# A curvature-flow stage on one core: another split of its small steps between the engines

## The chip, the cores and the metric

The kernel runs on 1 core of a Trainium2 chip. The metric is the device time in microseconds (us), the median of the runs. TensorE (PE) multiplies 32-row blocks held in SBUF and adds into PSUM (`bank`, 8 banks), VectorE (DVE) and ScalarE (ACT) do elementwise work on both memories, GpSimd (POOL) does elementwise work on SBUF, and SyncE (SP) issues the DMAs.

## The reference

Four layers follow one another on a batch of 16 images with 16 channels of 32 x 32: an attention layer, two residual convolution layers, and the curvature flow that the change is about. Its part of the reference, cut:

```python
def step(u, _):                                  # 10 steps; c() clips to +-10
    ux, uy, uxx, uxy, uyy = _derivs(u)           # Sobel stencils, each through c()
    g2 = ux * ux + uy * uy
    denK = jnp.maximum(1.0 + g2, EPS)
    K = jnp.clip((uxx * uyy - uxy * uxy) / (denK * denK + EPS), -5.0, 5.0)
    denH = jnp.sqrt(1.0 + g2 + EPS)
    H = ((1.0 + uy * uy) * uxx - 2.0 * ux * uy * uxy + (1.0 + ux * ux) * uyy) / (2.0 * denH ** 3 + EPS)
    H = jnp.clip(H, -5.0, 5.0)
    u = u + DT * jnp.clip(alpha * K + beta * H, -1.0, 1.0)      # DT = 0.01
    return jnp.pad(u[:, :, 1:-1, 1:-1], ((0, 0), (0, 0), (1, 1), (1, 1)), mode='edge'), None
u, _ = jax.lax.scan(step, x, None, length=10)
return 0.7 * u + 0.3 * x
```

## The kernel before

Until about 412 us the kernel streams weights and does the attention and the convolutions; the change leaves that alone but for a few two-element constants. Then the flow runs. The images are cut by channels into 4 chunks (`NCH`), each a tile `u[c]` of 128 partitions (4 channels of 32 image rows) by 34 x 16 columns (image column, batch). 10 steps of 4 chunks make 40 **slots**. A slot's inner part has 30 x 16 = 480 columns (`NF`); where two fields are handled at once, an instruction has 960.

**TensorE.** A derivative is a sum of terms, each a 32 x 32 matrix (the vertical part) times a shifted view of `u` (the horizontal part). `stencil` (line 585) does one term as 4 matmuls on 4 of the array's 32 x 32 tiles; `add` (line 596) does the same for a pointwise sum. This text calls such a group of 4 a **round**. Round t reads partitions shifted by 32 t: t = 0 is `u` itself, t = 1 to 3 are copies `turned`, which SyncE makes by six DMAs per slot (`turn`, line 357) after the border columns of `u` are written. Rounds of one t use the same four tiles and follow one another; rounds of different t use different tiles. A slot has 22 rounds: UX 2 (t = 0), UY 3 and UXX 3 (t = 1), UXY 4 (t = 2), UYY 5 (t = 3), and 5 adds (t = 0): ONE, ONE, MINUS_TWO sum the numerator of H in the second bank of the slot's bank pair, where UX stood before; ALPHA and BETA sum the step in bank 7.

**Per slot on the other engines**, by the line numbers of the profile:
- DVE: clip of ux, uy (L930, 960 columns), clip of the step in two instructions, L934 in PSUM and L939 with the addition to `u`, K's product `khk` (L944), clip of uxy (L947), H's product `khh` (L952), clip of uxx, uyy (L957, 960), `slope` = 1 + ux^2 + uy^2 (L961), `outer` (L963, 960).
- ACT: three squares (L1074 `p2`, L1075 `sqr` of 960, L1077 `sqxy`), the clip of H as two ramps (L1080, L1082), then the powers of the slope: Ln, Square, Exp (L1085, L1086, L1088), two Ln (L1090, L1092), two Exp (L1095 `invk`, L1097 `invh`).
- POOL: the products `cxy` (L1144), `m` (L1155), `cross` (L1158), `num` (L1161), the clip of K (L1147), and the copy of the two border columns of `u` (L1151), which SP waits for.

Every engine works its list in the order written; a slot's work is spread over iterations k, k+1 and k+2 of `slot_step` (new, old, older). After the loop, `edge` matmuls (L683) and `finish` (L981, L985) form 0.7 u + 0.3 x.

## Time and profile before

| | |
|---|---|
| median of 3 runs | 716.74 us (716.69 to 717.53) |
| the profiled execution, its own time | 716.67 us |
| span of its trace | 714.9 us |
| busy: PE, DVE, ACT, POOL | 643.1, 408.9, 328.2, 237.3 us |
| the flow, first stencil matmul to the end | 415.7 to 714.9 us |

In a timeline row stand the start and the duration in us, the engine, the line, the operation, the tiles written and read and their shape, and in brackets the idle time before it with the instruction that ended it. The start of one instruction to the start of the next on its engine is often shorter than the duration, as instructions overlap at their ends.

### The profile page before, as it was taken

How to read it: one execution, taken by the hardware profiler on the slowest of the kernel's cores; microseconds unless marked ns; L12 is line 12 of the kernel's file. 1: busy time of each engine (PE TensorE's matmuls, PEld its weight loads, DVE VectorE, ACT ScalarE, POOL GpSimd, SP SyncE). 2: the span in 40 equal slices, each digit the busy share in tenths (PEclk: the TensorE clock that was granted, in tenths of full speed). 3: DMA queues.
4: the chain of work that ended last, by engine and by line, in shares of the span. 5: the costliest groups of instructions: out<-in, count | busy, mean ns of one | idle time of the engine just before them, and what ended most of it. 6: DMA issues, size and time to landing. Idle time of an engine off the chain costs nothing.

```text
span 714.9 us, 22856 instructions
## 1 busy us (share of the span) xinstructions
PE 643.1 (90%) x10128; PEld 402.9 (56%) x10128; DVE 408.9 (57%) x635; ACT 328.2 (46%) x622; POOL 237.3 (33%) x250
## 2 busy tenths in 40 slices
...
GB/s 372 424 402 407 429 426 426 425 428 426 427 427 422 427 428 427 425 428 425 427 427 297 143 165 97 122 120 121 120 120 126 115 121 120 128 113 128 113 98 61
...
## 3 DMA queue, kind: packets, MB, share of 16 engines
...
q14 instruction: 11, 0.09, 0.0%
...
## 4 chain that ended last, share of the span: by engine, by line
PE 69%; DMA 25%; DVE 4%; issue 1%; ACT 1%; SPq 0%; DVEq 0%; ACTq 0%
PE bank L592 29%; DMA ring<-wout_w 15%; PE bank L600 11%; PE bank L402 8%; PE bank L418 7%; PE bank L526 4%; PE bank L471 4%; DMA ring<-wqk_p 3%; DMA ring<-wout_p 3%; DMA ring<-wv_w 3%; PE bank L552 3%; DMA xw<-x_window 1%; PE bank L557 1%; DVE reg_g L709 1%; PE bank L445 1%
## 5 line engine op out<-in xcount | busy, mean ns | idle before, releaser
L592 PE MATMUL bank<-ring 32*32 32x480 f32 x4800 | 283.5, 568 | 1.3 <-DMA ring<-reg_a 1.3
L600 PE MATMUL bank<-ring 32*32 32x480 f32 x1600 | 186.2, 564 | 1.2 <-ACT ring L1082 0.8
L592 PEld LDWEIGHTS bank<-ring 32*32 32x32 f32 x4800 | 125.3, 103 | 39.4 <-issue 25.7
L1144 POOL TENSOR_TENSOR ring<-ring 128x480 f32<-128x480 f32 x40 | 48.8, 1221 | 175.1 <-DVE ring L930 175.1
L418 PE MATMUL bank<-ring,small 128*32 128x256 f32 x1152 | 79.5, 424 | 30.3 <-DMA ring<-wout_w 24.6
L600 PEld LDWEIGHTS bank<-ring 32*32 32x32 f32 x1600 | 77.8, 104 | 37.0 <-issue 11.4
L418 PE MATMUL bank<-ring,xw 128*32 128x256 f32 x1024 | 62.8, 405 | 12.9 <-DMA ring<-wv_w 12.9
L418 PEld LDWEIGHTS bank<-ring,small 128*32 128x32 f32 x1152 | 39.6, 119 | 60.9 <-issue 22.3
L1155 POOL TENSOR_TENSOR ring<-ring 128x480 f32<-128x480 f32 x40 | 48.6, 1215 | 56.9 <-DVE ring L957 56.9
L765 DVE SCALAR_TENSOR_TENSOR reg_a<-bank,prm 128x512 f32<-128x512 f32 x4 | 2.8, 691 | 101.4 <-PE bank L478 101.4
L402 PE MATMUL bank<-reg_a,ring 128*128 128x256 f32 x256 | 57.9, 388 | 2.8 <-DMA ring<-wqk_p 2.0
L418 PEld LDWEIGHTS bank<-ring,xw 128*32 128x32 f32 x1024 | 33.8, 116 | 40.2 <-DMA ring<-wv_w 16.2
L402 PEld LDWEIGHTS bank<-reg_a,ring 128*128 128x128 f32 x256 | 49.6, 195 | 11.3 <-DMA ring<-wqk_p 2.9
L592 PE MATMUL bank<-reg_a,ring 32*32 32x480 f32 x480 | 55.3, 566 | 0.0
L1122 POOL MEMSET reg_d<- 128x2176 f32 x1 | 1.9, 1914 | 147.4 <-PE bank L478 147.4
L914 DVE STREAM_TRANSPOSE reg_b<-bank 128x256 f32<-128x256 f32 x16 | 7.2, 450 | 75.8 <-PE bank L418 75.8
L1158 POOL TENSOR_TENSOR ring<-ring 128x480 f32<-128x480 f32 x40 | 48.7, 1218 | 0.0
L1161 POOL TENSOR_TENSOR ring<-ring 128x480 f32<-128x480 f32 x40 | 48.7, 1217 | 0.0
L930 DVE TENSOR_SCALAR ring<-bank 128x960 f32<-128x960 f32 x40 | 45.8, 1146 | 3.7 <-PE bank L592 3.7
L957 DVE TENSOR_SCALAR ring<-bank 128x960 f32<-128x960 f32 x40 | 45.9, 1147 | 1.5 <-PE bank L592 1.5
L963 DVE SCALAR_TENSOR_TENSOR ring<-bank,ring 128x960 f32<-128x960 f32 x40 | 45.9, 1146 | 0.0
...
## 6 DMA issues: line engine op xcount, KB each, us to landing
...
ring<-reg_a SPq DMA_DIRECT2D x60, 136.0 KB, 2.5
...
```

The lines of the kernel that those rows point to most:

```text
L402: ins = te.matmul(bank[:, 4 + n % 2, (h % 2) * TOK:(h % 2 + 1) * TOK], half[2 * (k % NSLOT) + h // 4][:, c, h % 4 * DH:(h % 4 + 1) * DH], ...
L418: ins = te.matmul(bank[32 * j:32 * j + 32, b_, n0:n0 + 256], lhs(c), slot[k % NSLOT][:, c, 256 * j:256 * j + 256], start=start and c == 0, ...
L471: ins = te.matmul(bank[:, 4 + n % 2, :], fl[:, c, t * P:(t + 1) * P], half[2 * (kv % NSLOT) + h][:, c, :], start=(c == 0), stop=(c == KC - 1))
L592: last = te.matmul(bank[QUAD * j:QUAD * (j + 1), field, 0:NF], mat(m, (j + t) % NCH), whole[at_, 2 + off:S + off, :], start=(n == 0), stop ...
L600: last = te.matmul(bank[at_, to, 0:NF], mat(m, j), from_[at_, :], start=start, stop=stop, skip_group_check=True)
L930: v.tensor_scalar(two(f01[q]), pair(q), 10.0, -10.0, ALU.min, ALU.max).then_inc(ve["clip1"], 1)
L957: v.tensor_scalar(two(f34[q]), bank[:, OUTER:OUTER + 2, 0:NF], 10.0, -10.0, ALU.min, ALU.max).then_inc(ve["clip2"], 1)
L963: v.scalar_tensor_tensor(two(ab[q]), pair(q), 1.0, two(f34[q]), ALU.add, ALU.mult).then_inc(ve["outer"], 1)
L1144: p.tensor_tensor(cxy[q], f01[q][:, 0:NF], f01[q][:, NF:2 * NF], ALU.mult).then_inc(po["cxy"], 1)
L1155: p.tensor_tensor(mxy[q], f34[q][:, 0:NF], f34[q][:, NF:2 * NF], ALU.mult).then_inc(po["m"], 1)
L1158: p.tensor_tensor(cross[q], cxy[q], mix[q], ALU.mult).then_inc(po["cross"], 1)
L1161: p.tensor_tensor(num[q], mxy[q], sqm[q], ALU.subtract).then_inc(po["num"], 1)
```

## The change

All of it is in the flow. TensorE takes the x derivative UX from the copy with t = 2 instead of `u` itself; its rounds, and the instructions of all engines, stand in a new order, in which uxx, uxy's second half and uyy of a slot fall in the iteration behind its ux and uy. The clip of the step moves from DVE's L934 to two ScalarE ramps (`low` out of PSUM, `high` back into it), the clip of H from two ScalarE ramps to one GpSimd instruction, ScalarE's two logarithms become one of 960 columns, and the border copy moves from GpSimd to a `tensor_copy` on VectorE. The loops of VectorE and ScalarE are written out. The diff, cut: the old bodies are those printed above, so only new lines stand here, without the renamed semaphores and constants.

```diff
@@ a name for a position in the order
+class Slot:
+    def __init__(self, k):
+        self.k, self.q, self.live = k, k % 2, 1 <= k <= SLOTS
+        self.i, self.c = (k - 1) // NCH, (k - 1) % NCH
+        self.first = self.i == 0
@@ TensorE: slot_step(k), lines 603-665 replaced
+now, old, older = Slot(k), Slot(k - 1), Slot(k - 2)
+if old.live:
+    te.wait_ge(ld_turn[2][old.c], 32 * (old.i + 1))
+    if old.k > 1:
+        te.wait_ge(ve["clip2"], old.k - 1)
+    stencil(OUTER + 1, old, 3, UYY, 0)
+    stencil(MIXED, old, 2, UXY, 2)
+    if old.k > 1:
+        te.wait_ge(ve["clip2"], old.k - 1)
+    stencil(OUTER, old, 1, UXX, 0)
+    stencil(MIXED, old, 2, UXY, 3).then_inc(pe["fldxy"], 1)
+if older.live:
+    te.wait_ge(ve["outer"], older.k)
+    add(bank_set(older.q) + 1, ONE, ab[older.q][:, 0:NF], True, False)
+if old.live:
+    stencil(OUTER + 1, old, 3, UYY, 1)
+if older.live:
+    add(bank_set(older.q) + 1, ONE, ab[older.q][:, NF:2 * NF], False, False)
+if old.live:
+    stencil(OUTER + 1, old, 3, UYY, 2)
+    stencil(OUTER, old, 1, UXX, 1)
+if older.live:
+    te.wait_ge(po["cross"], older.k)
+    add(bank_set(older.q) + 1, MINUS_TWO, cross[older.q], False, True).then_inc(pe["hn"], 1)
+if old.live:
+    stencil(OUTER + 1, old, 3, UYY, 3)
+if now.live:
+    te.wait_ge(ld_turn[1][now.c], 32 * (now.i + 1))
+    if now.k > 1:
+        te.wait_ge(ve["clipxy"], now.k - 1)
+    stencil(MIXED, now, 2, UXY, 0)
+if old.live:
+    stencil(OUTER, old, 1, UXX, 2)
+    stencil(OUTER + 1, old, 3, UYY, 4).then_inc(pe["fld2"], 1)
+if now.live:
+    stencil(MIXED, now, 2, UXY, 1)
+    te.wait_ge(ld_turn[0][now.c], 32 * (now.i + 1))
+    if now.k > 2:
+        te.wait_ge(ve["khk"], now.k - 2)
+    stencil(bank_set(now.q), now, 1, UY, 0)
+if older.live:
+    te.wait_ge(po["clip_k"], older.k)
+    if older.k > 1:
+        te.wait_ge(ve["u"], older.k - 1)
+    add(STEP, ALPHA, clip_k[older.q], True, False)
+if now.live:
+    if now.k > 2:
+        te.wait_ge(ve["khh"], now.k - 2)
+    elif now.k == 2:
+        te.wait_ge(ac["u_in"], 2)
+    stencil(bank_set(now.q) + 1, now, 2, UX, 0)
+    stencil(bank_set(now.q), now, 1, UY, 1)
+if older.live:
+    te.wait_ge(po["clip_h"], older.k)
+    add(STEP, BETA, clip_h[older.q], False, True).then_inc(pe["step"], 1)
+if now.live:
+    stencil(bank_set(now.q) + 1, now, 2, UX, 1)
+    stencil(bank_set(now.q), now, 1, UY, 2).then_inc(pe["fld1"], 1)
@@ VectorE: lines 895-899
-then(v.tensor_scalar(dt_ab, prm[:, COL["alpha"][0]:COL["beta"][1]], DT, None, ALU.mult))
-then(v.tensor_scalar(five_ab, dt_ab, 5.0, None, ALU.mult))
-then(v.tensor_scalar(ten_ab, five_ab, 2.0, None, ALU.mult))
-then(v.tensor_scalar(neg_b, dt_ab[:, 1:2], -1.0, None, ALU.mult))
-v.tensor_tensor(mid, five_ab[:, 0:1], five_ab[:, 1:2], ALU.add).then_inc(ve["scales"], 1)
+v.tensor_scalar(dt_ab, prm[:, COL["alpha"][0]:COL["beta"][1]], DT, None, ALU.mult).then_inc(ve["scales"], 1)
@@ VectorE: slot_step(k), lines 923-963 replaced
+now, old, older = Slot(k), Slot(k - 1), Slot(k - 2)
+if old.live:
+    v.wait_ge(ac["p2"], old.k)
+    v.wait_ge(ac["sqr"], old.k)
+    v.scalar_tensor_tensor(slope[old.q], pair(old.q)[:, 1, :], 1.0, p2[old.q], ALU.add, ALU.add).then_inc(ve["slope"], 1)
+    v.wait_ge(pe["fld2"], old.k)
+    v.tensor_scalar(two(f34[old.q]), bank[:, OUTER:OUTER + 2, 0:NF], 10.0, -10.0, ALU.min, ALU.max).then_inc(ve["clip2"], 1)
+    v.wait_ge(ve["clip2"], old.k)
+    v.scalar_tensor_tensor(two(ab[old.q]), pair(old.q), 1.0, two(f34[old.q]), ALU.add, ALU.mult).then_inc(ve["outer"], 1)
+if now.live:
+    v.wait_ge(pe["fld1"], now.k)
+    v.tensor_scalar(two(f01[now.q]), pair(now.q), 10.0, -10.0, ALU.min, ALU.max).then_inc(ve["clip1"], 1)
+    v.wait_ge(pe["fldxy"], now.k)
+    v.tensor_scalar(mix[now.q], bank[:, MIXED, 0:NF], 10.0, -10.0, ALU.min, ALU.max).then_inc(ve["clipxy"], 1)
+if older.live:
+    v.wait_ge(ac["high"], older.k)
+    if older.first:
+        v.wait_ge(ac["x3"], older.k)
+    inner = u[older.c][:, 2 * B:S * B]
+    v.scalar_tensor_tensor(inner, bank[:, STEP, 0:NF], DT, inner, ALU.subtract, ALU.add).then_inc(ve["u"], 1)
+if old.live:
+    v.wait_ge(po["num"], old.k)
+    v.wait_ge(ac["invk"], old.k)
+    v.tensor_tensor(kh[old.q][:, 0:NF], num[old.q], pair(old.q)[:, 0, :], ALU.mult).then_inc(ve["khk"], 1)
+if older.live:
+    if older.k <= SLOTS - NCH:
+        v.wait_ge(ve["u"], older.k)
+        image_ = u3(older.c)
+        v.tensor_copy(image_[:, 1:S + 1:S - 1, :], image_[:, 2:S:S - 3, :]).then_inc(ve["pad"], 1)
+if old.live:
+    v.wait_ge(pe["hn"], old.k)
+    v.wait_ge(ac["invh"], old.k)
+    v.tensor_tensor(kh[old.q][:, NF:2 * NF], pair(old.q)[:, 1, :], inv_h[old.q], ALU.mult).then_inc(ve["khh"], 1)
@@ VectorE: lines 988-994 replaced (the Fori loop goes)
+for k in range(1, SLOTS + 2):
+    slot_step(k)
+for x in range(NCH - 1):
+    finish(x)
+slot_step(SLOTS + 2)
@@ ScalarE: slot_step(k), lines 1069-1097 replaced
+now, old, older = Slot(k), Slot(k - 1), Slot(k - 2)
+if old.live:
+    a.wait_ge(ve["clip1"], old.k)
+    a.activation(pair(old.q), f01[old.q].rearrange("p (x n) -> p x n", x=2), ACT.Square).then_inc(ac["sqr"], 1)
+    a.wait_ge(ve["clipxy"], old.k)
+    a.activation(sqm[old.q], mix[old.q], ACT.Square).then_inc(ac["sqxy"], 1)
+    a.wait_ge(ve["slope"], old.k)
+    a.activation(lnw[old.q], slope[old.q], ACT.Ln, bias=D_EPS).then_inc(ac["lnw"], 1)
+    a.wait_ge(ve["slope"], old.k)
+    a.activation(den[old.q][:, 0:NF], slope[old.q], ACT.Square).then_inc(ac["psq"], 1)
+    a.wait_ge(ac["lnw"], old.k)
+    a.activation(den[old.q][:, NF:2 * NF], lnw[old.q], ACT.Exp, bias=LN2, scale=1.5).then_inc(ac["w15"], 1)
+if older.live:
+    a.wait_ge(pe["step"], older.k)
+    a.activation(low[older.q], bank[:, STEP, 0:NF], ACT.Relu, bias=DT, scale=-1.0).then_inc(ac["low"], 1)
+if old.live:
+    a.wait_ge(ac["psq"], old.k)
+    a.wait_ge(ac["w15"], old.k)
+    a.activation(den[old.q], den[old.q], ACT.Ln, bias=D_EPS).then_inc(ac["ln"], 1)
+if older.live:
+    a.wait_ge(ac["low"], older.k)
+    a.activation(bank[:, STEP, 0:NF], low[older.q], ACT.Relu, bias=2 * DT, scale=-1.0).then_inc(ac["high"], 1)
+if now.live:
+    a.wait_ge(ve["clip1"], now.k)
+    a.activation(p2[now.q], f01[now.q][:, 0:NF], ACT.Square).then_inc(ac["p2"], 1)
+if old.live:
+    a.wait_ge(ve["outer"], old.k)
+    a.wait_ge(ac["ln"], old.k)
+    a.activation(pair(old.q)[:, 0, :], den[old.q][:, 0:NF], ACT.Exp, scale=-1.0).then_inc(ac["invk"], 1)
+    a.wait_ge(ac["ln"], old.k)
+    a.activation(inv_h[old.q], den[old.q][:, NF:2 * NF], ACT.Exp, scale=-1.0).then_inc(ac["invh"], 1)
@@ ScalarE: lines 1108-1114 replaced (the Fori loop goes)
+for k in range(1, SLOTS + 3):
+    slot_step(k)
@@ GpSimd: lines 1140-1161 replaced
+now, old = Slot(k), Slot(k - 1)
+if old.live:
+    p.wait_ge(ve["clipxy"], old.k)
+    p.wait_ge(po["cxy"], old.k)
+    p.tensor_tensor(cross[old.q], cxy[old.q], mix[old.q], ALU.mult).then_inc(po["cross"], 1)
+    p.wait_ge(ve["clip2"], old.k)
+    p.tensor_tensor(mxy[old.q], f34[old.q][:, 0:NF], f34[old.q][:, NF:2 * NF], ALU.mult).then_inc(po["m"], 1)
+    p.wait_ge(ac["sqxy"], old.k)
+    p.wait_ge(po["m"], old.k)
+    p.tensor_tensor(num[old.q], mxy[old.q], sqm[old.q], ALU.subtract).then_inc(po["num"], 1)
+if now.live:
+    p.wait_ge(ve["clip1"], now.k)
+    p.tensor_tensor(cxy[now.q], f01[now.q][:, 0:NF], f01[now.q][:, NF:2 * NF], ALU.mult).then_inc(po["cxy"], 1)
+if old.live:
+    p.wait_ge(ve["khk"], old.k)
+    p.tensor_scalar(clip_k[old.q], kh[old.q][:, 0:NF], 5.0, -5.0, ALU.min, ALU.max).then_inc(po["clip_k"], 1)
+    p.wait_ge(ve["khh"], old.k)
+    p.tensor_scalar(clip_h[old.q], kh[old.q][:, NF:2 * NF], 5.0, -5.0, ALU.min, ALU.max).then_inc(po["clip_h"], 1)
+for k in range(1, SLOTS + 2):
+    slot_step(k)
@@ SyncE: line 371
-sp.wait_ge(po["pad"], i * NCH + (c + 1 - NCH))
+sp.wait_ge(ve["pad"], i * NCH + (c + 1 - NCH))
```

## Rows read from the trace of the kernel before

**Rows 1.** Busy time by engine, 540 to 580 us: length, PE, PEld, DVE, ACT, POOL, PEclk, DMA.

```profile
540.00:580.00 40.00, 40.00 (x1008) 26.00 (x998) 38.42 (x53) 37.73 (x69) 31.05 (x34) 1.00 0.44 115
```

**Rows 2.** Timeline of PE, one slot: first UX pass, first ALPHA pass, last MINUS_TWO pass.

```profile
543.66 0.60 PE L592 MATMUL bank<-reg_a,ring 32*32 32x480 f32 x4
...
545.27 0.61 PE L600 MATMUL bank<-ring 32*32 32x480 f32 x4
...
549.32 0.59 PE L600 MATMUL bank<-ring 32*32 32x480 f32 x2
```

**Rows 3.** Timeline of DVE, the same slot.

```profile
542.86 0.66 DVE L952 TENSOR_TENSOR ring<-bank,ring 128x480 f32<-128x480 f32 x1 [0.23 <-PE bank L600]
543.43 1.15 DVE L957 TENSOR_SCALAR ring<-bank 128x960 f32<-128x960 f32 x1
544.50 0.65 DVE L961 SCALAR_TENSOR_TENSOR ring<-bank,ring 128x480 f32<-128x480 f32 x1
545.06 1.15 DVE L963 SCALAR_TENSOR_TENSOR ring<-bank,ring 128x960 f32<-128x960 f32 x1
...
547.19 0.72 DVE L934 TENSOR_SCALAR bank<-bank,small 128x480 f32<-128x480 f32 x1
547.94 0.66 DVE L939 SCALAR_TENSOR_TENSOR reg_a<-bank,reg_a 128x480 f32<-128x480 f32 x1
548.52 0.64 DVE L944 TENSOR_TENSOR ring<-ring,bank 128x480 f32<-128x480 f32 x1
```

**Rows 4.** Timeline of ACT, the same slot.

```profile
545.18 0.60 ACT L1085 ACTIVATE ring<-ring 128x480 f32<-128x480 f32 x1 [0.39 <-DVE ring L961]
...
548.65 0.59 ACT L1074 ACTIVATE ring<-ring 128x480 f32<-128x480 f32 x1
549.14 0.95 ACT L1075 ACTIVATE bank<-ring 128x960 f32<-128x960 f32 x1
550.04 0.59 ACT L1077 ACTIVATE ring<-ring 128x480 f32<-128x480 f32 x1
```

**Rows 5.** Timeline of POOL, the same slot.

```profile
544.66 1.21 POOL L1155 TENSOR_TENSOR ring<-ring 128x480 f32<-128x480 f32 x1 [1.36 <-DVE ring L957]
545.83 1.21 POOL L1158 TENSOR_TENSOR ring<-ring 128x480 f32<-128x480 f32 x1
...
549.48 0.59 POOL L1147 TENSOR_SCALAR ring<-ring 128x480 f32<-128x480 f32 x1
550.14 0.25 POOL L1151 TENSOR_TENSOR reg_a<-reg_a,ones 128x32 f32<-128x32 f32 x1
```

**Rows 6.** Timeline at 243 us: short DVE instructions beside a GpSimd memset.

```profile
242.87 1.80 POOL L1138 MEMSET reg_g<- 128x2048 f32 x1 [0.18 <-DVE xw L882]
243.10 1.60 DVE L895 TENSOR_SCALAR small<-prm 128x2 f32<-128x2 f32 x1
244.73 0.17 DVE L896 TENSOR_SCALAR small<-small 128x2 f32<-128x2 f32 x1
```

**Rows 7.** Timeline: the flow's first and last slot.

```profile
414.76 0.60 SPq L362 DMA_DIRECT2D ring<-reg_a  x1
...
424.96 0.60 ACT L1085 ACTIVATE ring<-ring 128x480 f32<-128x480 f32 x1 [2.61 <-DVE ring L961]
...
701.32 0.60 ACT L1085 ACTIVATE ring<-ring 128x480 f32<-128x480 f32 x1 [0.39 <-DVE ring L961]
...
703.80 0.55 ACT L1095 ACTIVATE bank<-ring 128x480 f32<-128x480 f32 x1
...
704.45 0.66 DVE L944 TENSOR_TENSOR ring<-ring,bank 128x480 f32<-128x480 f32 x1 [0.78 <-ACT bank L1095]
...
704.95 2.68 PE L683 MATMUL bank<-reg_a,ring 128*128 128x480 f32 x6
...
710.20 0.66 DVE L939 SCALAR_TENSOR_TENSOR reg_g<-bank,reg_g 128x480 f32<-128x480 f32 x1
```

**Rows 8.** DMA issues of the page: tiles, count, size, us from issue to landing.

```profile
ring<-reg_a SPq DMA_DIRECT2D x60, 136.0 KB, 2.5
```

More of the change, by code:

```diff
@@ L199, in build @@
         dst = sm(TOK // 4)
-        dt_ab, five_ab, ten_ab = (sm(2) for _ in range(3))
-        neg_b, mid = (sm(1) for _ in range(2))
+        dt_ab = sm(2)
         wft = sm(KC * 2 * B)
@@ L215, in build @@
             "pl_sq_sums", "pln", "negmax", "prob", "pf", "dsl", "stage", "conv", "bank_turn", "img",
-            "clip1", "clipxy", "clip2", "slope", "outer", "khk", "khh", "clipd", "u", "scales", "mats", "fin", "halo", "u_in", "band")}
+            "clip1", "clipxy", "clip2", "slope", "outer", "khk", "khh", "u", "pad", "scales", "mats", "fin", "halo", "u_in", "band")}
         ac = {n: sem("ac_" + n) for n in (
             "order", "patch_sq", "patch_std", "fl", "win_sq", "win_std", "pl_std", "qkv", "vt", "exp", "pt", "rows",
-            "wwk", "wv", "conv", "p2", "sqr", "sqxy", "lnw", "psq", "w15", "lnk", "lnh", "invk", "invh", "low_h", "clip_h", "x3",
+            "wwk", "wv", "conv", "p2", "sqr", "sqxy", "lnw", "psq", "w15", "ln", "invk", "invh", "low", "high", "x3",
             "halo", "u_in")}
-        po = {n: sem("po_" + n) for n in ("zero", "bandz", "padz", "cxy", "m", "num", "cross", "clip_k", "pad")}
+        po = {n: sem("po_" + n) for n in ("zero", "bandz", "padz", "cxy", "m", "num", "cross", "clip_k", "clip_h")}
         st_image, ld_u = sem("st_image"), [sem(f"ld_u{c}") for c in range(NCH)]
@@ L583, in _, with stencil @@
                 ins.then_inc(pe["chunk"], 1)
[L585 removed]
+            def stencil(field, a, t, terms, n):
                 off, m = terms[n]
[L588 to L589 removed]
+                m = MATS.index(m) + (0 if a.first else len(MATS))
+                whole = (u[a.c] if t == 0 else turned[:, t - 1, a.c, :]).rearrange("p (w b) -> p w b", b=B)
                 for j in range(NCH):
```

172 lines of the change are left out of this document (4 added, 168 removed).

## The prediction

> **What bounds the kernel now.** I read three views in this order: busy time by stage, the timeline of one slot engine by engine, and the chain of waits at its ends. In the flow PE shows 40.00 of 40 us busy and DVE 38.42, ACT 37.73, POOL 31.05 [rows 1]; a busy matmul queue proves little, but the timeline says what it is made of. The slot's first UX pass starts at 543.66 and its first ALPHA pass at 545.27 [rows 2]. Between them lie the four passes of UX's two rounds, so a round on one group of tiles is two passes of 0.40 us, 0.80 us in all. All seven t = 0 rounds (UX, UX, ALPHA, BETA, ONE, ONE, MINUS_TWO) follow one another on the same four tiles, until the last pass at 549.32 [rows 2], which is 14 passes and one slipped place after the first. It ends at 549.91; that is what `khh` waits for: its row of one slot before stands at 542.86 with 0.23 us idle, released by PE's L600 [rows 3]. `khh` ends at 543.52, and 0.14 later UX starts, whose bank the numerator of H had held. So the period is a ring: seven t = 0 rounds with a slip and the last pass's drain, 6.25, one `khh` 0.66, two hand-overs 0.18, together 7.09. Over the stage: L1085 of the first slot at 424.96, of the last at 701.32 [rows 7], 276.36 / 39 = 7.086 us a slot. DVE, idle only 0.23 of it, stands right behind.
>
> **What the change does to each engine.** Prices are the spacings of starts. *DVE* (960 columns: 543.43 to 544.50, 1.07; 480 columns: 0.56 to 0.58; one that needs the result just before it waits for the end, as L934 to L939, 0.75 at a duration of 0.72, so +0.03 [rows 3]): L934 goes, -0.75. The border copy comes; no row shows it on DVE. Below stands a DVE instruction of two columns, 0.17 [rows 6], above GpSimd's own copy, 0.25 [rows 5], and beside a running GpSimd instruction far more (below). I take 0.17, of which 0.05 overlaps, as the two-column row is nearest. `outer` now follows `clip2` directly, 1.15 + 0.03. Sum: slope 0.56, clip2 1.18, outer 1.07, clip1 1.07, clipxy 0.56, u 0.58, khk 0.58, copy 0.12, khh 0.57 = 6.29, from 6.86. *ACT* (480: 548.65 to 549.14, 0.49; 960: 0.90 [rows 4]): two ramps for H go and two for the step come, two logarithms become one: 9 x 0.49 + 2 x 0.90 = 6.21. That the ramps read and write PSUM costs nothing by L1075 and L1095, which write it at these prices. *POOL* (1.17 a product, 0.66 a clip [rows 5]): 4 x 1.17 + 2 x 0.66 = 6.00, from 5.6. *PE*: t = 0 drops to 5 rounds, t = 2 rises to 6, as t = 1 has; 6 x 0.80 = 4.8 is the floor, and read in the new order with in-order starts the 22 rounds fall into 7 groups, 5.6. So all four engines want about 6, and the period is decided by the rings between them.
>
> **The ring that I take to be the longest.** I walk one slot with time 0 at the start of `lnw` (ACT's Ln of the slope). ACT then: psq 0.51, w15 1.0, low of the slot before 1.5, ln 2.0, high 2.9, p2 of the next slot 3.4, invk 3.9, invh 4.4, sqr of the next slot 4.9. `sqr` lasts 0.95 and `slope` needs it: a result of ACT reaches DVE 0.10 after its end (703.80 + 0.55 to 704.45 [rows 7]), slope lasts 0.65, ACT starts 0.03 after it (544.50 + 0.65 to 545.18 [rows 3, 4]). From sqr to the next lnw are thus 1.73, of which sqr and sqxy fill 1.39, and ACT waits 0.34. Period: 6.21 + 0.34 = 6.55, with the 0.51 after a wait and roundings 6.6. DVE, walked the same way, gives nearly the same: slope, clip2, outer, clip1 until p2 may start, 0.56 + 1.18 + 1.07 + 1.15 + 0.09 = 4.05, then p2, invk, invh, sqr, slope, 0.49 x 3 + 0.95 + 0.10 = 2.52; 6.57. All other rings of the walk are shorter: numerator (khh 0.57, slope 0.56, clip2 1.18, outer 1.15, to PE 0.14, six t = 0 passes 2.60, to DVE 0.04) 6.24; clipxy to slope to clip2 to UYY, UXY, UXY and back to clipxy, 6.1; BETA to fld1 to clip1, on through khh, GpSimd's clip of H, BETA, 6.1; its step through low, ln, high, p2, invk, khk, khh, 6.2. The copies are in time: DVE writes the border at 5.3, the fourth of six DMAs is issued 4 x 0.62 later and lands 2.5 after that [rows 8], at about 9.7 to 10.3, and by the walk UXY wants it at 10.55. **Period 6.6**, from 7.09.
>
> **The ends.** UX and UXY now open the flow and need the t = 2 copy, whose second half is issued at 414.76 [rows 7] and lands 2.5 later [rows 8]; four t = 2 rounds 3.4, clip1 1.15, p2's place 0.6, sqr 0.95, slope 0.75 with hand-overs put the first lnw at 424.4, against 424.96. At the end the numerator of the last slot moves from iteration 41 to 42, and that stands behind the three edge matmuls, 2.68 together [rows 7], of which the third waits for slot 39's `u` at 4.2. Counted from the last lnw: edges done 5.25, numerator 2.6, khh 8.6, H's clip 9.25, BETA 10.4, the two ramps 11.6, u 12.3. Before, u's row started at 710.20, 8.9 after the last lnw, and ended 9.5 after it [rows 7]. So the tail grows by 2.8, and from the last lnw to the end of the span are 714.9 - 701.32 + 2.8 = 16.4.
>
> **Sum**, against the profiled execution of 716.67 (0.07 under the median), which has 1.77 outside its span: 424.4 + 39 x period + 16.4 + 1.77 = 442.6 + 39 x period. With 6.6: **700.0 us**. Removing DVE's small constants at 243 us and the written-out loops I cost at nothing: DVE then waits for PE's weights, and the loop's end shows no period longer than the others.
>
> **A rule against the change: the lock between DVE and GpSimd.** At 243 us a GpSimd memset runs from 242.87 to 244.67. A DVE instruction of two columns, SBUF to SBUF, starts at 243.10 and takes 1.60, until just after the memset's end; the same form directly behind takes 0.17 [rows 6]. So such an instruction waits for GpSimd's running one. Every DVE instruction of the flow has at most one SBUF input beside PSUM, and takes the same 0.65 beside a product of GpSimd (L961, L944 [rows 3, 5]); the border copy would be the first of this sort. The Trainium skill, SBUF — State Buffer, section Who interferes with whom, has the rule: a VectorE copy that uses both port pairs and GpSimd hold them exclusively, and the later one waits for the whole of the other; the trace agrees, with the 1.60 us. In my walk the copy finds GpSimd idle: cxy ends at 4.8, the clip of K cannot start before khk ends, at 5.17 + 0.08 (L957's end to L1155's start [rows 3, 5]), and the copy starts at 5.1. The margin is 0.3 behind cxy and 0.14 ahead of the clip.
>
> **The rivals.** *(A) The copy loses that race.* If it takes the lock more than 0.14 later than the spacing says, the clip of K goes first, and the DVE walk becomes: 4.05, p2 0.49, invk 0.55 + 0.10, khk 0.72, clip 0.59, copy 0.12, khh 0.57 = 7.19. Then 442.6 + 39 x 7.19 = 723.0, slower than before. It decides from a period of 7.07 on. For it: the 1.60 us; against: the order of starts. *(B) PE slips.* Before, one pass in 14 slipped; the numerator's ring of 6.24 has 0.36 to spare. One slip, 6.64, changes nothing; two, 7.04, give 717.2, no difference. For it: every group of tiles is now equally loaded, and rounds start in order; against: PE has 1 us of slack. *(C) Hand-overs are shorter than I take them*, and DVE's own 6.29 is the period: 687.9. Against: ACT's wait for slope follows from durations, and those hold to 0.01. *(D) Only the PE part works*, since the step's ramps come late: low waits for BETA, and a lateness over 0.4 us goes into ACT's ring, 6.9 to 7.0, 711.7 to 715.6.
>
> **How the numbers follow.** Forecast 0.74 (period 6.4 to 6.85, 692 to 710); A 0.09; B 0.05; C 0.06; D 0.06. The range from 690 to 715 takes in the forecast's, D and part of C: 0.82. A measurement of this kernel can tell about 0.2%, 1.4 us, from no change. Faster: the forecast, C, D and a little of B, 0.87; same: most of B, 0.04; slower: A, 0.09.
>
> **What would show it.** Right: L1085's successor every 6.6 us; ACT idle some 0.3 ahead of it behind slope and nowhere else; DVE's copy under 0.25 us; PE without a wait for khh that lasts. The copy at 0.6 us or more shows A; khh waiting for L600 shows B; ACT idle ahead of `low` behind PE shows D; the tail is right if the numerator's last rounds stand behind the edge matmuls. Wrong altogether if the period is 7.07 or more.

## The result: 699.9 us, 2.4% faster

| | before | after |
|---|---|---|
| median, us | 716.76 (716.69 to 717.53) | 699.88 (699.19 to 700.91) |
| ratio after / before | | 0.9764, 95% interval 0.9751 to 0.9777 |
| profiled execution, us; its span | 716.67; 714.9 | 700.35; 698.5 |
| first Ln of the slope, us | 424.96 | 425.70 |
| last Ln of the slope, us | 701.32 | 682.31 |
| period of a slot, (last - first) / 39 | 7.086 | 6.580 |
| last Ln to end of span | 13.5 | 16.2 |

Between the two profiled executions the gain is 39 x 0.506 = 19.7 us in the periods, less 0.7 in the fill and 2.7 in the tail: 16.3 us of span. The line numbers from here on are those of the kernel after (`slope` L928, `clip2` L930, `outer` L932, `clip1` L935, `clipxy` L937, `u` L943, `khk` L947, border copy L952, `khh` L956; ACT: `sqr` L1065, `sqxy` L1067, `lnw` L1069, `low` L1076, `ln` L1080, `high` L1083, `p2` L1086; PE: stencil passes L597, the sums L605, edges L685).

Busy time by engine of the kernel after, the stage and the fill (us and count for PE, PEld, DVE, ACT, POOL; granted clock; DMA). The first line answers to [rows 1]:

```profile
540.00:580.00 40.00, 40.00 (x1089) 21.32 (x1081) 38.89 (x56) 38.41 (x67) 36.24 (x38) 1.00 0.52 133
416.00:418.00 2.00, 1.07 (x16) 0.51 (x20) 0.00 (x0) 0.00 (x0) 0.00 (x0) 0.77 0.76 205
418.00:420.00 2.00, 2.00 (x25) 0.81 (x17) 0.00 (x0) 0.00 (x0) 0.00 (x0) 0.50 0.82 227
420.00:422.00 2.00, 2.00 (x45) 1.47 (x38) 0.00 (x0) 0.00 (x0) 0.00 (x0) 0.87 0.76 218
```

DVE and ACT are as busy as before, but over a shorter slot; POOL rose from 31.05 to 36.24. Timeline of DVE of the kernel after, one slot (start, us, instruction, idle time before it), which answers to [rows 3]:

```profile
541.64 0.65 DVE L943 SCALAR_TENSOR_TENSOR reg_a<-bank,reg_a 128x480 f32<-128x480 f32 x1
542.36 0.65 DVE L947 TENSOR_TENSOR ring<-ring,bank 128x480 f32<-128x480 f32 x1
542.93 0.17 DVE L952 COPY reg_a<-reg_a 128x32 f32<-128x32 f32 x1
543.02 0.65 DVE L956 TENSOR_TENSOR ring<-bank,ring 128x480 f32<-128x480 f32 x1
543.75 0.66 DVE L928 SCALAR_TENSOR_TENSOR ring<-bank,ring 128x480 f32<-128x480 f32 x1
544.32 1.15 DVE L930 TENSOR_SCALAR ring<-bank 128x960 f32<-128x960 f32 x1
545.50 1.16 DVE L932 SCALAR_TENSOR_TENSOR ring<-bank,ring 128x960 f32<-128x960 f32 x1
546.58 1.15 DVE L935 TENSOR_SCALAR ring<-bank 128x960 f32<-128x960 f32 x1
```

`khh` starts 0.09 after the copy: nothing holds it any more, where before it waited 0.23 for PE. The copy takes 0.17. The only late starts are `slope`, 0.73 after `khh` instead of 0.57, and `khk`, which follows `u` after 0.72 instead of 0.57: some 0.15 each, behind `sqr` and `invk` of ACT.

Timeline of ACT of the kernel after, one slot, which answers to [rows 4]:

```profile
542.69 0.95 ACT L1065 ACTIVATE bank<-ring 128x960 f32<-128x960 f32 x1
543.59 0.59 ACT L1067 ACTIVATE ring<-ring 128x480 f32<-128x480 f32 x1
544.44 0.60 ACT L1069 ACTIVATE ring<-ring 128x480 f32<-128x480 f32 x1 [0.27 <-DVE ring L928]
...
545.93 0.55 ACT L1076 ACTIVATE ring<-bank 128x480 f32<-128x480 f32 x1
...
547.77 0.59 ACT L1086 ACTIVATE ring<-ring 128x480 f32<-128x480 f32 x1
...
551.00 0.60 ACT L1069 ACTIVATE ring<-ring 128x480 f32<-128x480 f32 x1 [0.27 <-DVE ring L928]
```

Ln to Ln is 6.56, and the only idle time is the 0.27 ahead of it, behind `slope` (0.36 if counted by starts: `sqxy` to Ln is 0.85, where such a step is 0.49 elsewhere). Timeline of POOL of the kernel after, which answers to [rows 5]:

```profile
541.58 1.22 POOL L1143 TENSOR_TENSOR ring<-ring 128x480 f32<-128x480 f32 x1
543.10 0.59 POOL L1146 TENSOR_SCALAR ring<-ring 128x480 f32<-128x480 f32 x1 [0.30 <-DVE ring L947]
...
545.61 1.23 POOL L1137 TENSOR_TENSOR ring<-ring 128x480 f32<-128x480 f32 x1
546.98 1.22 POOL L1140 TENSOR_TENSOR ring<-ring 128x480 f32<-128x480 f32 x1
```

The product before the copy ends at 542.80, the copy starts at 542.93 and ends at 543.10, where the clip of K starts. That is the gap the forecast relied on, 0.13 wide on its left side. Timeline of the kernel after, fill and tail, which answers to [rows 7]:

```profile
416.93 7.55 PE L597 MATMUL bank<-ring 32*32 32x480 f32 x116 [2.59 <-DMA ring<-reg_a]
...
422.24 1.16 DVE L935 TENSOR_SCALAR ring<-bank 128x960 f32<-128x960 f32 x1 [7.56 <-PE bank L597]
...
682.31 0.60 ACT L1069 ACTIVATE ring<-ring 128x480 f32<-128x480 f32 x1 [0.27 <-DVE ring L928]
...
686.55 1.04 PE L685 MATMUL bank<-reg_a,ring 128*128 128x480 f32 x2 [1.26 <-DVE reg_a L943]
687.52 3.42 PE L605 MATMUL bank<-ring 32*32 32x480 f32 x32
...
690.21 0.66 DVE L956 TENSOR_TENSOR ring<-bank,ring 128x480 f32<-128x480 f32 x1 [3.25 <-PE bank L605]
```

In the tail the last numerator stands behind the edge matmuls, as walked. In the fill PE waits 2.59 us for the turned copy, and then runs at a granted clock of 0.50 (1.2 GHz).

### The profile page after: what moved, and what is told of

It reads as the page before. It is cut to its first block, busy times and chain, and to the rows that moved or that the text cites. A ratio compares the mean times of both kernels' runs of the same rounds, so it can differ in the third digit from the quotient of the medians.

```text
span 698.5 us, 22687 instructions
## 1 busy us (share of the span) xinstructions
PE 624.1 (89%) x10128; PEld 362.1 (52%) x10128; DVE 389.5 (56%) x627; ACT 314.6 (45%) x582; POOL 253.5 (36%) x254
## 4 chain that ended last, share of the span: by engine, by line
DVE 36%; PE 31%; DMA 26%; ACT 3%; issue 3%; SPq 0%; DVEq 0%; POOLq 0%; POOL 0%; ACTq 0%
DMA ring<-wout_w 16%; PE bank L407 8%; PE bank L423 7%; DVE ring L932 6%; DVE ring L935 6%; DVE ring L930 6%; PE bank L531 4%; PE bank L476 4%; DVE ring L928 4%; DMA ring<-wqk_p 3%; DVE ring L937 3%; DMA ring<-wv_w 3%; DMA ring<-wout_p 3%; DVE ring L956 3%; PE bank L557 3%
## 5 line engine op out<-in xcount | busy, mean ns | idle before, releaser
L597 PE MATMUL bank<-ring 32*32 32x480 f32 x5440 | 264.7, 570 | 2.6 <-DMA ring<-reg_a 2.6
L605 PE MATMUL bank<-ring 32*32 32x480 f32 x1600 | 177.3, 566 | 0.6 <-POOL ring L1148 0.6
L597 PEld LDWEIGHTS bank<-ring 32*32 32x32 f32 x5440 | 135.8, 103 | 70.9 <-issue 56.1
L1143 POOL TENSOR_TENSOR ring<-ring 128x480 f32<-128x480 f32 x40 | 48.9, 1223 | 178.5 <-DVE ring L935 178.5
L423 PE MATMUL bank<-ring,small 128*32 128x256 f32 x1152 | 81.6, 433 | 29.5 <-DMA ring<-wout_w 23.7
L605 PEld LDWEIGHTS bank<-ring 32*32 32x32 f32 x1600 | 42.3, 104 | 56.9 <-issue 21.9
L1140 POOL TENSOR_TENSOR ring<-ring 128x480 f32<-128x480 f32 x40 | 48.5, 1212 | 5.7
L935 DVE TENSOR_SCALAR ring<-bank 128x960 f32<-128x960 f32 x40 | 45.9, 1147 | 7.7 <-PE bank L597 7.6
L1137 POOL TENSOR_TENSOR ring<-ring 128x480 f32<-128x480 f32 x40 | 48.8, 1221 | 0.9 <-DVE ring L930 0.9
L932 DVE SCALAR_TENSOR_TENSOR ring<-bank,ring 128x960 f32<-128x960 f32 x40 | 46.3, 1157 | 1.4
L930 DVE TENSOR_SCALAR ring<-bank 128x960 f32<-128x960 f32 x40 | 45.9, 1148 | 0.1
L1080 ACT ACTIVATE ring<-ring 128x960 f32<-128x960 f32 x40 | 39.7, 992 | 0.1
```

The source lines that it names most:

```text
L423: ins = te.matmul(bank[32 * j:32 * j + 32, b_, n0:n0 + 256], lhs(c), slot[k % NSLOT][:, c, 256 * j:256 * j + 256], start=start and c == 0, ...
L597: last = te.matmul(bank[QUAD * j:QUAD * (j + 1), field, 0:NF], mat(m, (j + t) % NCH), whole[at_, 2 + off:S + off, :], start=(n == 0), stop ...
L605: last = te.matmul(bank[at_, to, 0:NF], mat(m, j), from_[at_, :], start=start, stop=stop, skip_group_check=True)
L930: v.tensor_scalar(two(f34[old.q]), bank[:, OUTER:OUTER + 2, 0:NF], 10.0, -10.0, ALU.min, ALU.max).then_inc(ve["clip2"], 1)
L932: v.scalar_tensor_tensor(two(ab[old.q]), pair(old.q), 1.0, two(f34[old.q]), ALU.add, ALU.mult).then_inc(ve["outer"], 1)
L935: v.tensor_scalar(two(f01[now.q]), pair(now.q), 10.0, -10.0, ALU.min, ALU.max).then_inc(ve["clip1"], 1)
```

## Experiments

All times are against runs of the kernel before on the same chip (716.8 to 716.9).

| run | median, us (range) | ratio, 95% interval | period, us |
|---|---|---|---|
| x1: x derivative from `u` itself | 728.52 (726.79 to 729.02) | 1.0155, 1.0129 to 1.0182 | 7.30 |
| x2: before, x derivative from the turned copy | 728.53 (728.27 to 729.63) | 1.0157, 1.0129 to 1.0185 | 7.39 |
| x3: border copy ahead of `khk` | 713.42 (712.75 to 715.08) | 0.9951, 0.9935 to 0.9966 | 6.94 |
| x4: step's clip on DVE | 713.43 (712.53 to 713.56) | 0.9940, 0.9920 to 0.9961 | 6.93 |
| x5: squares split | 695.48 (695.02 to 697.07) | 0.9709, 0.9694 to 0.9724 | 6.46 |
| x6: x5, `p2` last | 692.13 (691.47 to 693.19) | 0.9656, 0.9641 to 0.9671 | 6.35 |
| x7: last slot's sums ahead of an edge | 698.34 (697.52 to 698.67) | 0.9738, 0.9725 to 0.9751 | 6.57 |
| x8: UY opens the flow | 699.27 (698.53 to 701.15) | 0.9757, 0.9743 to 0.9772 | 6.57 |
| x9: x6, x7 and x8 together | 688.86 (688.57 to 690.29) | 0.9607, 0.9591 to 0.9623 | 6.34 |
| x10: border copy on GpSimd | 700.80 (698.72 to 701.63) | 0.9779, 0.9763 to 0.9795 | 6.57 |
| x11: PE kept busy in the fill | 699.64 (one run) | | 6.57 |

The periods are medians of the spacing of one instruction in the profiled execution.

### What the PE part does: x1 and x2

x1 is the kernel after with only UX put back on `u`, that is on the t = 0 tiles (and it waits for the border copy):

```diff
-                    stencil(bank_set(now.q) + 1, now, 2, UX, 0)
+                    stencil(bank_set(now.q) + 1, now, 0, UX, 0)
...
-                    stencil(bank_set(now.q) + 1, now, 2, UX, 1)
+                    stencil(bank_set(now.q) + 1, now, 0, UX, 1)
```

> The changed kernel, but UX is taken from u itself (t = 0) again, with a wait for the border copy: the t = 0 tiles carry 7 rounds, as before the change. Ring theory: no ring of the new order runs through all seven of them; fld1 comes 0.8 us later and clip1 has 0.9 to spare, so the period stays at 6.58 to 6.7 and the time at 700 to 705. Rival, that the gain came from unloading the t = 0 tiles: the old period, 7.09, some 719.

Measured: 728.52, slower than before, which neither theory had. The timelines of x1 (POOL, PE and DVE rows of one slot; here L1148 is the clip of K, L937 `clip1`, L949 `khk`) show a ring that I had not walked:

```profile
546.07 0.59 POOL L1148 TENSOR_SCALAR ring<-ring 128x480 f32<-128x480 f32 x1 [0.65 <-DVE ring L949]
...
546.71 0.60 PE L605 MATMUL bank<-ring 32*32 32x480 f32 x4
...
547.53 0.98 PE L597 MATMUL bank<-reg_a,ring 32*32 32x480 f32 x8
548.34 0.58 PE L605 MATMUL bank<-ring 32*32 32x480 f32 x4
...
549.55 0.58 PE L597 MATMUL bank<-reg_a,ring 32*32 32x480 f32 x4
...
550.26 1.16 DVE L937 TENSOR_SCALAR ring<-bank 128x960 f32<-128x960 f32 x1 [0.64 <-PE bank L597]
```

ALPHA waits for the clip of K and starts at 546.71. ALPHA, UX's first round (547.53), BETA (548.34) and UX's second round (last passes at 549.55) have the same four tiles, so they run one after another, 3.55 until `clip1` at 550.26. From there `clip1` 1.08, `clipxy` 0.56, `u` 0.72 (until `khk`, which waits for ACT's `invk`), `khk` 0.65, 0.08 to the clip of K, 0.59 and 0.06 lead to the next ALPHA: 7.30. With UX on the t = 2 tiles, UX need not stand behind ALPHA and BETA. That is what the turned copy does for the new order, more than the lower number of t = 0 passes: the 14 passes of 0.40 in x1 are 5.6 of the 7.30.

x2 does the PE part alone, in the kernel before, with a wait for the turned copy in place of that for the border columns:

```diff
-                    if not first:
-                        te.wait_ge(po["pad"], k - NCH)
+                    te.wait_ge(ld_turn[1][c], 32 * (i + 1))
...
-                    stencil(ux, c, 0, first, UX, 0)
+                    stencil(ux, c, 2, first, UX, 0)
...
-                    stencil(ux, c, 0, first, UX, 1).then_inc(pe["fld1"], 1)
+                    stencil(ux, c, 2, first, UX, 1).then_inc(pe["fld1"], 1)
```

> The kernel before, with one part of the change alone: UX from the copy with t = 2. Ring theory: from khh over UX to the numerator and back to khh falls from 7.09 to 6.6, and DVE's own 6.86 is the period; 716.8 - 39 x 0.23 = 708 (706 to 711). Rival, that PE's order or the hand-over at khh binds whatever tiles UX uses: 716 to 717.

Measured: 728.53; here too both theories failed, and the sign with them. Timelines of x2 (PEld, PE and DVE; L592 is the stencil, L600 the sums, L951 `khh`):

```profile
541.60 0.21 PEld L592 LDWEIGHTS bank<-ring 32*32 32x32 f32 x16 [0.67 <-issue]
...
542.49 0.77 PE L600 MATMUL bank<-ring 32*32 32x480 f32 x4
...
543.24 1.04 PE L592 MATMUL bank<-ring 32*32 32x480 f32 x13
...
547.56 0.61 PE L600 MATMUL bank<-ring 32*32 32x480 f32 x4
547.74 1.44 PE L592 MATMUL bank<-ring 32*32 32x480 f32 x20
...
548.21 0.66 DVE L951 TENSOR_TENSOR ring<-bank,ring 128x480 f32<-128x480 f32 x1 [0.36 <-PE bank L600]
```

The ring from `khh` to `khh` over PE is still the one that binds, with the same wait behind L600. But the last sum's last pass starts 5.93 after UX's first (547.56 against 541.63, which is 0.03 behind its weight load), where before it was 5.66 [rows 2], although two rounds fewer stand on the t = 0 tiles: five rounds, 10 passes of 0.40, want 4.0. Before, these tiles had no pause, as 14 passes and one slipped place make up the 5.66. Here they have one. ALPHA's input and its tiles are free from 540.8 on, but it starts only at 542.49, within 0.01 of UX's second round, which is on other tiles; and from there the ten passes take 5.1 until the last one starts, where one every 0.40 would take 3.6.

Now UX, UX and UXY open the slot on one group of tiles, the first 1.6 us start few passes (32), and the rest comes bunched: from 543.24 to 547.74, 124 passes start, one every 36 ns. Single passes start within 10 ns of one another, but over any 64 in a row the closest mean spacing is 28.7 ns in the kernel before and 32 in the kernel after. By the 28.7 the 176 passes of a slot (22 rounds of 8) would take 5 us, and 6.3 by the 36 of this slot, where 16 passes every 0.40 would be 4.4. So two things keep a round waiting that a count of passes per group does not have: it can wait while its own tiles are free, and many passes at once start further apart than their tiles ask for. What makes either is not settled.

Program order alone does not make it. Timeline of PE of the kernel before, from the slot of [rows 2]; the rows that read `reg_a` are UX's:

```profile
543.75 0.81 PE L592 MATMUL bank<-ring 32*32 32x480 f32 x8
544.15 0.81 PE L592 MATMUL bank<-ring 32*32 32x480 f32 x8
544.47 0.61 PE L592 MATMUL bank<-reg_a,ring 32*32 32x480 f32 x4
```

Between the start of UX's first round (543.66) and that of its second (544.47), 16 other passes start, which are two rounds. The program has one there, UY's third. The other is UXY's first, which the program puts behind UX's second: its tiles were free, UX's were not, and it went ahead. So the prediction's "in-order starts" do not hold, and that every engine works its list in the order written is not so for PE's starts. The Trainium skill, TensorE: Matmul & The Clock Gate, section The mechanism (Packing small matmuls), says that matmuls start and end in program order, without reordering; these starts do not agree.

### The lock between DVE and GpSimd: x3 and x10

x3 puts the border copy one place earlier, straight behind `u`, where the walk has GpSimd still in the product of L1143:

```diff
-                if old.live:
-                    v.wait_ge(po["num"], old.k)
-                    v.wait_ge(ac["invk"], old.k)
-                    v.tensor_tensor(kh[old.q][:, 0:NF], num[old.q], pair(old.q)[:, 0, :], ALU.mult).then_inc(ve["khk"], 1)
                 if older.live:
...
                         v.tensor_copy(image_[:, 1:S + 1:S - 1, :], image_[:, 2:S:S - 3, :]).then_inc(ve["pad"], 1)
                 if old.live:
+                    v.wait_ge(po["num"], old.k)
+                    v.wait_ge(ac["invk"], old.k)
+                    v.tensor_tensor(kh[old.q][:, 0:NF], num[old.q], pair(old.q)[:, 0, :], ALU.mult).then_inc(ve["khk"], 1)
```

> The changed kernel with the border copy ahead of khk on DVE, where GpSimd's product cxy runs. Lock theory: the copy waits for the end of cxy, its row shows 0.4 us or more in place of 0.17, and cxy, copy, khk, clip of K, clip of H, cross, m, num, cxy become a ring of about 7.1; 716 to 722. Without a lock: the copy stays at 0.17, khk starts 0.05 later at most; 700 to 702.

Measured: 713.42, between the two. Timelines of x3 (POOL's product, DVE's copy at L948, and what follows it):

```profile
546.29 1.23 POOL L1143 TENSOR_TENSOR ring<-ring 128x480 f32<-128x480 f32 x1
...
546.84 0.72 DVE L948 COPY reg_a<-reg_a 128x32 f32<-128x32 f32 x1
547.48 0.64 DVE L952 TENSOR_TENSOR ring<-ring,bank 128x480 f32<-128x480 f32 x1
```

The same copy takes 0.72, until just after the product's end (547.52), instead of 0.17. So the lock is there, and one place in the order is worth 13.5 us. My sum for it was too long: the copy lengthens DVE's list by 0.55, and as it needs the result just ahead of it, `u` takes 0.68 until it instead of 0.57; with 6.24 (x4, below) that makes 6.90, and the period is 6.94.

x10 does the same copy on GpSimd, behind that product, as a multiplication by ones as before:

```diff
+                    p.tensor_tensor(image_[:, 1:S + 1:S - 1, :], image_[:, 2:S:S - 3, :],
+                                    ones[:, 0:2 * B].rearrange("p (x b) -> p x b", x=2), ALU.mult).then_inc(po["pad"], 1)
...
-                        v.tensor_copy(image_[:, 1:S + 1:S - 1, :], image_[:, 2:S:S - 3, :]).then_inc(ve["pad"], 1)
```

> The changed kernel with the border copy on GpSimd again, ahead of the clip of K. Ring theory: DVE's list gets 0.12 shorter but the rings through ACT stay at 6.58, and GpSimd's list grows from 6.2 to 6.6; period 6.58 to 6.65, 700 to 703. Rival, that DVE's list is the bound: 39 x 0.12 less, 695.

Measured: 700.80, no difference. ACT still waits 0.27 ahead of `lnw` (L1064 here; timeline of ACT):

```profile
549.34 0.60 ACT L1064 ACTIVATE ring<-ring 128x480 f32<-128x480 f32 x1 [0.27 <-DVE ring L928]
```

So moving the copy to VectorE earns nothing by itself; it only must not meet a running GpSimd instruction.

### The step's clip: x4

x4 clips the step on DVE again and takes the two ramps from ACT:

```diff
-                    v.wait_ge(ac["high"], older.k)
+                    v.wait_ge(pe["step"], older.k)
+                    v.tensor_scalar(bank[:, STEP, 0:NF], bank[:, STEP, 0:NF], DT, -DT, ALU.min, ALU.max).then_inc(ve["clipd"], 1)
+                    v.wait_ge(ve["clipd"], older.k)
...
-                    v.scalar_tensor_tensor(inner, bank[:, STEP, 0:NF], DT, inner, ALU.subtract, ALU.add).then_inc(ve["u"], 1)
+                    v.scalar_tensor_tensor(inner, bank[:, STEP, 0:NF], 0.0, inner, ALU.add, ALU.add).then_inc(ve["u"], 1)
...
-                    a.activation(low[older.q], bank[:, STEP, 0:NF], ACT.Relu, bias=DT, scale=-1.0).then_inc(ac["low"], 1)
...
-                    a.activation(bank[:, STEP, 0:NF], low[older.q], ACT.Relu, bias=2 * DT, scale=-1.0).then_inc(ac["high"], 1)
```

> The changed kernel with the step's clip as one instruction on DVE again (in PSUM, as before) and without the two ScalarE ramps. Ring theory: DVE's list grows by 0.75 to 7.04 and is the period; 699.9 + 39 x 0.46 = 718 (715 to 720), the whole gain gone though PE and its order are the new ones. Rival, that TensorE's tiles and order made the gain: 700 to 704.

Measured: 713.43. Timeline of DVE of x4, `clip1` of two slots and the clip:

```profile
538.99 1.15 DVE L935 TENSOR_SCALAR ring<-bank 128x960 f32<-128x960 f32 x1
...
540.62 0.66 DVE L940 TENSOR_SCALAR bank<-bank 128x480 f32<-128x480 f32 x1
541.31 0.66 DVE L945 SCALAR_TENSOR_TENSOR reg_g<-bank,reg_g 128x480 f32<-128x480 f32 x1
...
545.92 1.15 DVE L935 TENSOR_SCALAR ring<-bank 128x960 f32<-128x960 f32 x1
```

DVE runs without a gap: 6.93 a slot, of which the clip is 0.69. So DVE's list without it is 6.24, and the step's clip, put back on DVE by itself, costs 13.5 of the 17 us (the parts need not add: x1 costs more than all). I had expected 718, from a list of 6.29 and a clip of 0.75; the list is shorter by 0.05 and the clip, as one instruction, by 0.06. The move of the clip of H and the single logarithm were not undone by themselves.

### Is it ACT's ring over `slope`? x5 and x6

x5 squares the half that `slope` reads first, as an instruction of its own, so that the other half fills the wait:

```diff
-                    v.wait_ge(ac["sqr"], old.k)
+                    v.wait_ge(ac["sqr"], 2 * old.k - 1)
...
+                    v.wait_ge(ac["sqr"], 2 * old.k)
...
-                    a.activation(pair(old.q), f01[old.q].rearrange("p (x n) -> p x n", x=2), ACT.Square).then_inc(ac["sqr"], 1)
+                    for half in (1, 0):
+                        a.activation(pair(old.q)[:, half, :], f01[old.q][:, half * NF:(half + 1) * NF], ACT.Square).then_inc(ac["sqr"], 1)
```

> The changed kernel, but the square of 960 columns is two of 480, ux first, and slope waits for that one alone. Ring theory: ACT's wait of 0.27 ahead of the logarithm goes, ACT's list is 6.29, and the period falls to the next ring (slope, clip2, outer, clip1, p2, invk, khk, copy, khh), 6.46; 699.9 - 39 x 0.12 = 695 (694 to 698). Rival, that DVE's or PE's list is the bound: no change, or 39 x 0.08 = 3 us slower by the extra ACT instruction.

Measured: 695.48, as expected. Busy time by engine of x5:

```profile
540.00:580.00 40.00, 40.00 (x1102) 24.28 (x1091) 38.93 (x57) 39.98 (x76) 36.78 (x38) 1.00 0.50 131
```

No idle time of ACT is left (39.98 of 40), although its list is 0.09 longer. By starts, `p2` and Ln together are still some 0.15 late, where it was 0.36 ahead of Ln; the overlap of instructions hides that from the idle time. x6 also moves `p2` behind `invh`, so that a late `clip1` no longer stops ACT there:

```diff
-                if now.live:
-                    a.wait_ge(ve["clip1"], now.k)
-                    a.activation(p2[now.q], f01[now.q][:, 0:NF], ACT.Square).then_inc(ac["p2"], 1)
...
                     a.activation(inv_h[old.q], den[old.q][:, NF:2 * NF], ACT.Exp, scale=-1.0).then_inc(ac["invh"], 1)
+                if now.live:
+                    a.wait_ge(ve["clip1"], now.k)
+                    a.activation(p2[now.q], f01[now.q][:, 0:NF], ACT.Square).then_inc(ac["p2"], 1)
```

> As the one before, and p2 stands behind the two exponentials on ACT. Ring theory: no ring runs through clip1, p2 and invk any more; DVE's list 6.29, ACT's 6.29 and GpSimd's 6.2 are left; period 6.3 to 6.4, 689 to 693. Rival, DVE's or PE's list bound already: 700 to 703.

Measured: 692.13, as expected. The two together show that the rings through `sqr`, `slope` and `p2` set the period after the change, not one engine's list.

### The ends: x7, x8, x10 and x11

x7 hands out the last slot's sums one place earlier, ahead of the edge matmuls of the third piece:

```diff
             for x in range(NCH):
-                if x == NCH - 1:
+                if x == NCH - 2:
                     slot_step(SLOTS + 2)
```

> The changed kernel with PE's last iteration (numerator and step of slot 40) ahead of the third edge matmul. Tail theory: the numerator no longer waits behind an edge that waits for slot 39's u, khh of slot 40 comes 2.2 us earlier, the end 1.8 to 2.3 us earlier; 697.6 to 698.1. If the numerator's place in the tail costs nothing: 699.9.

Measured: 698.34, 1.5 less and 0.2 above what I expected. `khh` of the last slot follows 5.6 after the last Ln in x7, 7.9 in the kernel after (690.21 - 682.31); the pieces behind it take some of that back, and from the last Ln to the end of the span it is 14.4 against 16.2.

x8 opens the flow with UY, whose t = 1 copy lands first:

```diff
+                if k == 1:
+                    te.wait_ge(ld_turn[0][0], 32)
+                    for n in range(3):
+                        stencil(bank_set(1), now, 1, UY, n)
+                    te.wait_ge(ld_turn[1][0], 32)
+                    stencil(bank_set(1) + 1, now, 2, UX, 0)
...
```

> The changed kernel, but in the first slot alone PE starts with UY, whose copy lands first, then UX, then UXY. Fill theory: PE starts some 1.3 us earlier, has no wait of 2.6 us, its granted clock stays at 1.00, and the first clip comes at 418.7 in place of 422.2; 3.4 us less, 696.5 (696 to 697.5). Rival, that the next slots then wait for their copies: 698 to 700.

Measured: 699.27; the rival came true. Timeline of x8 (DVE's `clipxy` and `clip2` of the first slot, PE's late copy near the end):

```profile
422.27 0.66 DVE L947 TENSOR_SCALAR ring<-bank 128x480 f32<-128x480 f32 x1 [1.99 <-PE bank L597]
...
424.39 1.16 DVE L940 TENSOR_SCALAR ring<-bank 128x960 f32<-128x960 f32 x1 [0.90 <-PE bank L597]
...
660.37 1.64 PE L597 MATMUL bank<-ring 32*32 32x480 f32 x32 [0.51 <-DMA ring<-reg_a]
```

Its first `clip1` starts at 419.12, 3.1 earlier, but `clipxy` and `clip2` then wait for PE, and the second slot's `slope` is only 1.33 earlier, at a granted clock of 1.00; x11, below, has 1.46 at that clock with the old opening, so the new one is worth nothing. The 1.33 hold until slot 37; there a turned copy came late, once, and took half of it back.

x11 gives PE three matmuls whose result nobody reads, in the wait of the fill:

```diff
             te.wait_ge(ve["mats"], 2)
+            for _ in range(3):
+                te.matmul(bank[:, 3, :], ones[:, :], prm[:, 0:512], start=True, stop=True)
```

> The changed kernel with three matmuls of 128 x 128 x 512, results unused, in PE's wait ahead of the first slot. Clock theory: the granted clock of 0.77 and 0.50 at 416 to 420 us follows from PE's 2.6 us without work; with work it stays at 1.00, and the first clip starts at about 420.9 in place of 422.2. Rival, that the first rounds are slow for another reason (the DMA traffic, the start of the 32 x 32 tiles): 422.2 again.

Measured: 699.64 in one run. The granted clock is 1.00 throughout the fill, and every `slope` from the second to the 40th starts 1.46 earlier than in the kernel after. Busy time by engine of x11, the fill, then its last microseconds:

```profile
418.00:420.00 2.00, 2.00 (x50) 1.29 (x46) 0.00 (x0) 0.00 (x0) 0.00 (x0) 1.00 0.76 233
...
694.00:695.00 1.00, 1.00 (x3) 0.43 (x2) 0.49 (x2) 0.00 (x0) 0.00 (x0) 0.50 0.00 0
```

50 passes at 1.00, 25 at 0.50 in the kernel after. But x11's last edge matmuls fall into a stretch at 0.50 and take 1.94 for what the kernel after does in 1.05 at 1.00, so the span is only 0.7 shorter. Timeline of x11:

```profile
693.23 1.94 PE L687 MATMUL bank<-reg_g,ring 128*128 128x240 f32 x4 [2.08 <-DVE reg_g L945]
```

Both kernels waited 2.08 ahead of these matmuls. Behind the same wait of 2.08 they take 1.94 in x1, x3, x5 and x6 too, and 1.05 in x8 and x10. Nor do the extra matmuls prove themselves in the fill: x10, which has the opening of the kernel after unchanged, waited 2.85 for the copy and then ran at 1.00 (first `clip1` at 420.77, as in x11 at 420.78; 422.24 in the kernel after). Over the profiled executions with that opening, the clock fell in the kernel after, x4 and x7 (waits of 2.59 to 2.85) and stayed in x3, x5, x6 and x10 (2.56 to 2.95). So the runs show what the lower clock costs, some 1.5 us in the fill and 0.9 at the end, and that the wait's length alone does not decide whether it comes. What does is open. Both are as large as the differences of x7 and x8 in the table, so those two are read from their places in the traces.

### A faster version: x9

x9 takes x6, x7 and x8 together.

> The squares split, p2 last, the last sum ahead of the third edge and UY opening, together in the changed kernel. Each acts on another place (period, tail, fill), so the gains add: 8 to 11 us, 2 us and 3.4 us; 684 to 687. Rival: the shorter period lets the copies or PE come late, and less than half of it is left.

Measured: 688.86, 1.6% less than the kernel after and the fastest of all; yet 2 us above what I expected. Busy time by engine, and the waits of PE's weight loads for a turned copy (us in total, times, longest), of x9:

```profile
540.00:580.00 40.00, 40.00 (x1123) 25.68 (x1107) 39.27 (x56) 40.00 (x77) 37.60 (x39) 1.00 0.54 140
```

```profile
PEld bank L597 <- DMA ring<-reg_g: 2.3, 3, 1.0
```

ACT is the bound: 40.00 of 40 busy, 6.34 a slot, where its list is 6.29 (11 starts of 0.49 and one of 0.90). PE's weight loads wait for a turned copy in `reg_g` three times and for one in `reg_a` five times, 1.6 in all. Set against those of the kernel after, the starts of `slope` come 0.22 earlier with each slot, but lose 0.75, 0.3 and 0.6 of it at three slots, 1.7 in all. With the shorter period the copies have lost some of their slack; x6 shows it too, with 0.24 and 1.0 lost at two slots. Larger is the miss by x8's part, put in at 3.4: the last `slope` stands 8.5 ahead of that of the kernel after in x9 and 8.6 in x6. What x9 has over x6 is the tail, 14.7 against 17.0 from the last Ln, of which 0.9 is x6's lower clock at its end.

## Why the prediction was right, and where not

**The sum.** Against the profiled execution: first Ln 424.4 forecast, 425.70 measured; 39 periods 257.4 (6.6), 256.6 (6.580); tail 16.4, 16.2; outside the span 1.77, 1.85. 700.0 against 700.35. Its terms held within 1.3. That the sum is off by only 0.35 is luck in part: the fill took 1.3 more than forecast, the periods 0.8 and the tail 0.2 less.

**The ring over `sqr`, `slope` and `lnw`: right**, and shown. ACT waits ahead of `lnw` and nowhere else in the slot: 1.75 from `sqr` to `lnw` against 1.73, of which ACT stands still 0.36 by starts against 0.34. x5, which takes away more than half of that, gains 4.4 us. The walk on DVE gave nearly the same period, 6.57; its two waits of some 0.15 are there. DVE's list I had at 6.29; it is 6.24 (x4), in part because the copy adds 0.09 and not 0.12.

**The lock: right in mechanism, closer than I took it.** The copy meets no GpSimd instruction and takes 0.17, but 0.13 behind the product's end, not 0.3. GpSimd's list was the term mis-sized: L1140 needs L1137's result and starts 1.37 after it, where I had 1.17 for each product, so the list is 6.2 and not 6.00. x3 shows that the danger was real. Rival A priced the loss of the race with the clip of K; the loss that x3 tries, against the product, costs 13.5 us, and would still have been faster than before by 0.5%.

**PE: the kernel before read rightly, the step from there not.** The seven t = 0 rounds do fill their tiles before, one pass every 0.40 and one slipped place in the 5.66 of [rows 2]. But I took it that fewer of them make the ring shorter, and read PE after the change as 5.6 by groups with in-order starts, and a floor of 4.8. x2 takes two of those rounds off the group and becomes slower, as the sums start late and far apart; starts are not in order; and x1 shows a ring over ALPHA and BETA which I did not have among the walks. Rival D did not come about, since the ramps are in time; its name, "only the PE part works", is answered by x2, where the PE part alone gives 728.5. That the period after did not suffer from this is because UX, in its new place, stands behind nothing late. I had walked that without pricing what its absence would cost.

**The step's ramps** are in time: `low` starts directly behind its predecessor (545.93, 0.49 after it), without a wait for BETA.

**The fill: mis-sized by 1.3.** I counted four t = 2 rounds at 0.85. From PE's start to `clip1` the kernel after takes 5.31, at a granted clock that falls to 0.50; x10, at 1.00, takes 3.62 (417.15 to 420.77). By x10 and x11, at 1.00, `clip1` starts at 420.8, where the working has it (424.4 less 0.75, 0.95, 0.6 and 1.15 is 420.95). I had seen PE's wait for the t = 2 copy and priced it as time, and had no term for a lower clock behind it.

**The tail: right**, 16.2 against 16.4, with the numerator behind the edge matmuls; x7 shows that this order costs 1.5 us (1.8 from the last Ln to the end of its trace).
